# Attention over a context: the sum of a context's squares on TensorE behind the second scores, its copy behind two halves, the second root ahead of the scale

## The reference

```python
def _L0_xattn_ref(x, w1, w2):
    h = jnp.einsum('eth,efh->etf', x, w1)
    a = jax.nn.gelu(h, approximate=True)
    return jnp.einsum('etf,efh->eth', a, w2)
...
x = x + jnp.tanh(g_xattn[0]) * _L0_xattn_ref(_layernorm(x, axis=-1), ctx_1024, ctx_1024)
x = x + jnp.tanh(g_ffn[0]) * _L0_ffn_ref(_layernorm(x, axis=-1), L0_ffn_gate_w, L0_ffn_w1, L0_ffn_w2, L0_ffn_w3)
```

## Time and profile before

| what | us |
|---|---|
| median of 3 runs | 695.38 |
| lowest, highest | 694.34, 696.14 |
| the profiled execution, first to last instruction | 703.6 |
| attention loop in it | about 17 to 382 |
| expert phase in it | about 382 to 703 |

### The profile page before, as it was taken

How to read it: one execution, slowest core, us unless ns; L and a number is a source line. 1 busy time by engine, 2 the same in 40 slices (tenths; PEclk the granted TensorE clock), 3 DMA queues, 4 the chain that set the end, 5 groups by cost and what they waited for, 6 DMA issues and landing times.

```text
span 703.6 us, 15832 instructions
## 1 busy us (share of the span) xinstructions
PE 641.4 (91%) x4638; PEld 443.4 (63%) x4639; DVE 417.0 (59%) x1287; ACT 461.6 (66%) x771; POOL 403.9 (57%) x459
## 2 busy tenths in 40 slices
PE   2799999899999999999898999989999999999990
PEld 1677788777877877778785555444554555545550
DVE  3457878888778887797796644453333333333330
ACT  5999999998988989889874344334443444344440
POOL 4422545765666656665566586765555555555551
PEclk9999999999999999999999999999999999999996
DMA  7546557756586567655433566656665766666653
GB/s 213 148 142 188 153 155 155 197 139 183 137 188 160 163 141 195 168 150 166 121 102 88 102 121 115 97 91 119 117 109 106 118 113 109 115 116 115 112 105 55
DMA packets 51380, 94.77 MB, mean 135 GB/s; under 512 B 17024, under 2 KB 25344, under 8 KB 51312
## 3 DMA queue, kind: packets, MB, share of 16 engines
q1 hardware_dynamic: 34096, 60.02, 32.5%
q0 software_dynamic: 16400, 33.89, 27.0%
q10 hardware_dynamic: 816, 0.02, 0.1%
HBM read 61.89 MB, written 32.01 MB: 133 GB/s over the span
## 4 chain that ended last, share of the span: by engine, by line
DMA 24%; PE 12%; issue 6%; DVE 4%; POOL 2%; POOLq 1%; ACT 1%; DVEq 1%; SPq 0%; ACTq 0%
DMA out_rows<-ctx_raw,meta 21%; PE bank L1369 6%; PE bank L1378 3%; DMA ctx_raw<-xf_rows,meta 2%; POOL out_rows L537 2%; PE bank L1324 1%; POOLq L533 1%; PE bank L1358 1%; ACT ctx_raw L766 0%; DMA meta<-route_table 0%; PE bank L1258 0%; POOL ctx_raw L525 0%; PE bank L1223 0%; DVE ctx_part L825 0%; DVEq L1155 0%
## 5 line engine op out<-in xcount | busy, mean ns | idle before, releaser
L1369 PE MATMUL bank<-w,ctxT 128*128 x756 | 175.2, 382 | 0.9 <-issue 0.9
L537 POOL DMA_INDIRECT out_rows<-ctx_raw,meta x63 | 100.3, 1592 | 103.4 <-DMA out_rows<-ctx_raw,meta 91.2
L1223 PE MATMUL bank<-ctx_part,a_part 125*112 125x512 f16 x576 | 135.1, 380 | 0.1
L1211 PE MATMUL bank<-xnT,ctxT 128*125 128x224 f16 x1152 | 120.7, 262 | 2.4 <-DVE xnT L855 1.9
L1369 PEld LDWEIGHTS bank<-w,ctxT 128*128 128x128 f16 x756 | 74.3, 98 | 77.1 <-issue 3.4
L1211 PEld LDWEIGHTS bank<-xnT,ctxT 128*125 128x125 f16 x1152 | 112.2, 138 | 2.8 <-DVE xnT L855 2.2
L777 ACT ACTIVATE ctxT<-bank,cols 128x256 f32<-128x256 f32 x63 | 29.8, 473 | 121.6 <-issue 103.9
L1223 PEld LDWEIGHTS bank<-ctx_part,a_part 125*112 125x112 f16 x576 | 71.4, 130 | 39.1 <-DVE a_part L834 0.3
L629 ACT ACTIVATE ctxT<-bank 128x1000 f16<-128x1000 f16 x96 | 94.4, 1005 | 1.4 <-PE bank L1178 1.4
L1378 PE MATMUL bank<-w2s,ctxT 128*128 x378 | 91.9, 379 | 1.3 <-DVE ctxT L1138 1.3
L489 POOL DMA_INDIRECT route_table<-route,pos_i x64 | 72.7, 1136 | 19.2 <-issue 17.8
(11 more groups left out here) (155 smaller groups left out, 1026.4 us busy)
## 6 DMA issues: line engine op xcount, KB each, us to landing
ctx_raw<-in_ctx SPq DMA_DIRECT2D x48, 448.0 KB
w_raw<-in_L_ffn_w SPq DMA_DIRECT2D x24, 512.0 KB
x<-in_x SPq DMA_DIRECT2D x16, 448.0 KB, 6.5
out_rows<-x SPq DMA_DIRECT2D x16, 448.0 KB
xf_rows<-xf SPq DMA_DIRECT2D x16, 448.0 KB
ctx_raw<-in_ctx SPq DMA_DIRECT2D x48, 52.0 KB
meta<-route_table SPq DMA_DIRECT2D x66, 1.0 KB
ctx_raw<-xf_rows,meta POOLq DMA_INDIRECT x66
```

What stands on the lines that cost most here:

```text
L537: g.indirect_dma_start(out=out, out_offset=bass.IndirectOffsetOnAxis(ap=meta[n][:, 0:1], axis=0), in_=y_sb[n % 2], in_offset=None, compute ...
L1211: ins = t_.matmul(dst, ctxT[u][:, hc * KD + k, c * CS:c * CS + CR], xnT[u][:, hx, k, :], start=j == 0, stop=j == KD * len(PARTS) - 1)
L1223: ins = t_.matmul(O_ps[t][0:TT, :], a_part[ha][:, c, t * TT:(t + 1) * TT], ctx_part[u][hc][:, c, :], start=c == 0 and (ha, hc) == PARTS[0] ...
L1369: ins = t_.matmul(H_ps[u][:, :], rows, w, start=m == 0, stop=m == KD * len(PARTS) - 1)
```

## The change

Four programs are reordered, and nothing is added or removed. In steps 1 to 14:

- PE: the sum over partitions stands behind the second scores instead of between the first and the second.
- ACT: the copy of that sum stands behind the first two high halves instead of before them; the second gelu follows it.
- DVE: the factors stand behind norm 2 instead of behind the first low half.

On POOL, in every step but 0, the second root stands ahead of the scale instead of behind it.

```diff
--- before.py
+++ after.py
@@ -501,9 +501,9 @@
 
             def step(i, u, h):
                 two = not isinstance(i, int) or i + 2 < B
-                context_scale(i + 1)
                 if later(i, 1):
                     inv_std(mv2, 2, mv2_ready, rstd2_ready, i)
+                context_scale(i + 1)
                 inv_std(mv1, 0, mv1_ready, rstd1_ready, i + 2)
                 if later(i, 3):
                     send_routes(i - 3, 1 - u)
@@ -697,9 +697,9 @@
                     ctx_high_part(1, 1, 1)
                     act.wait_ge(table_ready, 48)
                 else:
-                    ctx_tot_out(i + 1)
                     ctx_high_part(i + 1, w, 0)
                     ctx_high_part(i + 1, w, 1)
+                    ctx_tot_out(i + 1)
                     gelu(i, u, 1)
                 split_end(weight_tot_out, i, u, h)
                 ctx_high_part(i + 1, w, 2)
@@ -973,13 +973,12 @@
                 if not later(i, 1):
                     a_low(i, u, 1)
                 context_low(i + 1, w, 0)
-                if later(i, 1):
-                    context_factors(i + 1, w)
                 if later(i, 3):
                     route_scores(i - 3, w)
                 if later(i, 1):
                     a_low(i, u, 1)
                     norm2(j)
+                    context_factors(i + 1, w)
                 split_end(weight_scale, i, u, h)
                 stats1(i + 1, w, (h + u) * 16 + 16)
                 context_low(i + 1, w, 1)
@@ -1281,9 +1280,9 @@
                 if not later(i, 1):
                     for c in range(2, NC):
                         trans_ctx(0, 0, c)
+                scores(i, u, 1)
                 if later(i, 1):
                     ctx_total(i + 1)
-                scores(i, u, 1)
                 if (i - 2) * S * TOPK == MAPPED:
                     counts(i - 2)
                 if later(i, 2):
```

## The result

The changed kernel takes 688.01 us (median of 4 runs, 687.02 to 688.32), the kernel before 695.05 us on the same chip: a ratio of 0.9900 (95% interval 0.9886 to 0.9914), 7.0 us less. On a second chip it was 687.33 against 693.9, 0.9901 (0.9884 to 0.9917). The forecast was 687.9, 7.5 us less.

What follows compares the result with a forecast made beforehand. The attention loop was taken as bound by a ring of engines waiting for each other, none saturated. Gains of 2.75 (even), 3.3 (odd) and 1.4 (early steps), total 7.5 us, off the 695.38 median gave 687.9; range 685.0 to 695.3.

Steps and rivals of the forecast that it cites:

- DVE: factors behind norm 2, 0.55 us a step: DVE in even steps: with the factors after norm 2, the weight scale starts 0.55 us earlier; five steps give 2.75.
- POOL's scale at its new place, 1.73 plus one block of up to 0.68: POOL's scale after the late copy: 1.73 us free plus at most 0.68 blocked by DVE, all_s between 210.15 and 210.85.
- the first rival: POOL's scale stays blocked by L834 and L877 at 2.86 us; each step gains only 0.15: 693.3 us; chance 0.17.
- ACT: no wait at the new place of the copy: ACT behind two halves: the sum is made some 2 us before the copy wants it, so ACT doesn't wait.
- The second root: POOL: moved ahead of the scale, it fills 0.92 us of idle time and is done 3 us sooner, by about 206.6.
- PE: 0.66 us in odd steps: PE with the sum moved: 0.66 of its 0.71 us idle time is usable in odd steps; five give 3.3.
- The early steps: Loop steps 1 to 4: estimated gains of 0.15, 0.48, 0.25 and 0.55 us, together 1.4.
- PE waits longer for xn in even steps: PE in even steps: its gain only turns into more of the 0.86 us wait for DVE's xn.
- The other signs: Profile after: DVE's wait before a_low not over 0.4 us, ACT's before L658 near 0.6 even, none odd; steps 22.8 and 21.4.
- Profiled span against median: Whole kernel: profiled 703.6 us against a median of 695.38, 1.2% more, was taken as nothing for terms of this size.
- The slower rival: POOL becomes the bound through the late copy: scale 3.56 us, seven even steps lose 3.9 us: 699.3 us; chance 0.08.

Runs made afterwards that it cites:

- DVE and POOL alone: Kernel before with only DVE's factors behind norm 2 and POOL's second root ahead of the scale; sum and copy in their old places: 690.55 us, 0.9952.
- PE and ACT alone: Kernel before with only PE's sum behind the second scores and ACT's copy behind two halves; DVE's and POOL's order as before: 714.75 us, 1.0300.

## Why the prediction was right

It was right in sign, size and split: 7.5 us, where the timed runs have 7.0 and 6.6 and the profiles 6.3. The term of the odd steps was mis-sized, and that of the early steps came out near by luck.

- **DVE: factors behind norm 2, 0.55 us a step.** Measured: even steps 22.87 to 22.32 from step 6 on. Right, and the run with DVE and POOL alone shows this term by itself.
- **POOL's scale at its new place, 1.73 plus one block of up to 0.68.** Measured 2.27, and 1.75 where it ran with DVE standing idle (PE and ACT alone). L443 came 0.31 us later beside a_low, and L444 grew by 0.17 beside L877; in the run where DVE stood idle neither did, so I read both as holds by DVE. A one-input operation did cost POOL something, then, but nowhere near the 1.13 us of holds that the first rival kept: it was refuted. The Trainium skill, "SBUF — State Buffer", section "Who interferes with whom", says that a VectorE instruction with two SBUF inputs contends with a GpSimd instruction that reads SBUF; the 0.31 us beside a_low agree. Of a hold by a tensor_scalar the trace shows 0.17 us.
- **ACT: no wait at the new place of the copy.** Right; with the copy at its old place ACT waited 2.5 us.
- **The second root.** Its worth isn't in the sum, only in the cover of norm 2. Without it the change is some 32 us slower, about 10 of them with the clock. I had the mechanism, not the size.
- **PE: 0.66 us in odd steps.** This term was mis-sized: 0.46. I took it from the idle time of 0.71 us before the sum, which belonged to the disturbed execution; the undisturbed one is 0.24. Counted from start to start, the first scores to the product with `gate` behind the second, step 10 shows what was gained (second profiles, before first):

```profile
243.14 2.49 PE L1211 MATMUL bank<-xnT,ctxT 128*125 128x224 f16 x24
...
246.12 2.49 PE L1211 MATMUL bank<-xnT,ctxT 128*125 128x224 f16 x24
248.45 1.65 PE L1258 MATMUL bank<-gate,xfT 128*112 128x8 f32 x16
```

```profile
240.78 4.79 PE L1210 MATMUL bank<-xnT,ctxT 128*125 128x224 f16 x48
...
245.56 1.72 PE L1257 MATMUL bank<-gate,xfT 128*112 128x8 f32 x16
```

  Before 5.31 us, after 4.78, 0.53 less; in step 9 the attend then starts 0.08 us later behind that product (1.58 instead of 1.50), and 0.45 is left. So more than the idle time was gained: I had written that PE gains its idle time "and pays nothing new", where in truth the sum's own exposed time was part of the gain. The 0.46 need the copy's move too: with the copy early they were 0.35.
- **The early steps.** I gave steps 1 to 4 0.15, 0.48, 0.25 and 0.55 us, 1.4 in all. They gained 0.23, -0.05, 0.46 and 0.61, 1.25 in all: the sum is near by luck. Step 2 gains nothing, since DVE has no route scores before step 3: it comes to a_low early, waits 1.03 us there for ACT's half (0.27 in step 8), and the factors behind norm 2 come on top. In all the profiles have 2.75 + 2.3 + 1.25 = 6.3 us, where the forecast had 2.75 + 3.3 + 1.4.
- **PE waits longer for xn in even steps.** Wrong: 0.86 before and 0.86 after (only in step 2 it grew, from 0.47). PE's gain there (about 0.45) and DVE's (0.55) are nearly the same size, so the wait stayed.
- **The other signs.** ACT's wait before the first weight is 0.53 us in even steps and gone in odd ones, and DVE's new wait before a_low is 0.27: as forecast. The steps are 22.3 and 20.9 us instead of 22.8 and 21.4, since those were counted from the lengths in the disturbed profile.
- **Profiled span against median.** The profile was 8 us above the median and I called that "nothing" on terms of this size. The two later profiles of before lie 1 to 3 us below it. It was the sign that the profile was disturbed, and the odd term came out of it.
- **The slower rival** was put at 0.08 and decided by a scale of 3.0 us or more. It didn't occur, but its mechanism, a late all_s ahead of DVE's chain, is what the three runs with a late copy and a covering move missing show. They cost 21 to 26 us, where I had worked out 3.9. With PE and ACT alone some 6 us of the 20.9 go with the clock and about 5 are lost in odd steps, where I had let PE's gain make up for the wait.

## What to carry to other kernels

A wait that is moved off one engine is paid by whoever stands behind the value that is now late; before moving it, list those consumers and move each behind work that doesn't need the value. Here the late copy without all of its covers costs 21 to 26 us, the covers without the late copy gain 3.4, and the whole change gains 7. If the profiled execution is more than a per cent off the median, take a second profile before pricing idle times of tenths of a microsecond.

## What was not expected of the hardware

TensorE's clock: with PE and ACT alone, in step 2, two waits of 0.93 and 0.87 us, with work on both sides of them, were followed by a stretch at granted clock 0.50, where six matmuls took 2.77 instead of 1.46 us. Steps 6, 8 and 10 of the same kernel had waits of 1.41 to 1.46 and 0.87 us and kept 1.00. Without POOL's move all seven even steps had waits of 1.43 to 1.72 and 0.86 us, and the clock fell in all seven. Single waits of 0.86 us an even step, as before and after the change, never brought it on in steps 1 to 14 of the five profiles. What decides between the cases isn't shown. So a wait of 1 us more on DVE cost up to 2.7 us in step 2 (22.28 us before, 25.01 with PE and ACT alone), and with DVE's old order 4.4 us in step 4 (23.17 and 27.59).

The forecast's "at granted clock 1.00" for the whole loop holds from step 1 on. In step 0, which the change doesn't touch, the first and third profile of before and the second of the changed kernel have a stretch at 0.50 (34 to 36 us), and the other two have none.
